# Graph network on one core: one-hots stored and loaded, maxima taken on 32 rows, the edge angle by TensorE, loops written out

## What is computed

```python
def transformer_conv(x, src, dst, edge_attr, Wq, bq, Wk, bk, Wv, bv, We, Wskip, bskip):
    ...
    e = (edge_attr @ We).reshape(-1, HEADS, C)
    k_j = k[src] + e
    v_j = v[src] + e
    alpha = jnp.einsum('ehc,ehc->eh', q[dst], k_j) / jnp.sqrt(jnp.float32(C))
    amax = jax.ops.segment_max(alpha, dst, num_segments=n)
    expa = jnp.exp(alpha - amax[dst])
    denom = jax.ops.segment_sum(expa, dst, num_segments=n)
    attn = expa / (denom[dst] + 1e-16)
    out = jax.ops.segment_sum(attn[:, :, None] * v_j, dst, num_segments=n)
...
rel_t = last_update[src] - t
rel_t_enc = jnp.cos(rel_t[:, None] * Wt[0][None, :] + bt)
edge_attr = jnp.concatenate([rel_t_enc, msg], axis=-1)
```

## Time and profile before

| | us |
| --- | --- |
| median of 3 runs | 13423.76 |
| lowest and highest | 13402.09, 13431.12 |
| span of the profiled execution | 13400.0 |
| preparation, to the first layer | 1505 |
| attention passes over the edges (four) | about 1150 each |
| gated pass over the edges | 1418 |
| convolution passes over the edges | 1673 and 1686 |

### The profile page before, as it was taken

One profiled execution on the slowest core, in us unless ns is written; L12 is line 12 of the kernel. 1 busy time (PEld: TensorE's weight loads), 2 busy tenths in 40 slices (PEclk: granted clock), 3 DMA queues, 4 the chain that ended last, 5 costly groups with the idle time before them and its releaser, 6 DMA issues. The chain is left out here.

```text
span 13400.0 us, 212567 instructions
## 1 busy us (share of the span) xinstructions
PE 8527.8 (64%) x52858; PEld 6962.8 (52%) x52859; DVE 10400.3 (78%) x15015; ACT 3614.6 (27%) x7819; POOL 6926.8 (52%) x7047
## 2 busy tenths in 40 slices
PE   4663477776777677775465652777266666567764
PEld 3553245554455535654455542555266666566664
DVE  8666569974799748996688875888778888688888
ACT  0111133332333233332244431333211111111111
POOL 2775047750477407772277750777145555255553
PEclk8555688877888788887688875666588888788887
DMA  4334754444544474443255550222233334233333
GB/s 182 113 113 119 244 206 106 106 80 193 192 106 106 72 292 123 106 106 53 79 145 145 146 111 19 55 55 54 19 103 106 107 107 105 75 108 105 105 106 72
DMA packets 720185, 1523.62 MB, mean 114 GB/s; under 512 B 364796, under 2 KB 416585, under 8 KB 680627
## 3 DMA queue, kind: packets, MB, share of 16 engines
q0 software_dynamic: 306624, 795.04, 25.0%
q1 hardware_dynamic: 413427, 727.07, 15.9%
HBM read 1050.48 MB, written 471.10 MB: 114 GB/s over the span
## 5 line engine op out<-in xcount | busy, mean ns | idle before, releaser
L970 POOL DMA_INDIRECT h<-table,edges_ring x3984 | 3856.5, 968 | 1889.0 <-issue 1154.3
L1147 PE MATMUL bank<-h,edges_onehot 128*128 128x260 f32 (+1 forms) x7968 | 1986.6, 406 | 652.3 <-issue 469.0
L1147 PEld LDWEIGHTS bank<-h,edges_onehot 128*128 128x128 f32 x7968 | 1570.6, 246 | 978.1 <-issue 717.4
L970 POOL DMA_INDIRECT edges_rows<-table,edges_ring x1512 | 1527.0, 1010 | 716.0 <-issue 431.0
L1122 PE MATMUL bank<-ident,edges_score 128*4 128x128 f32 x5280 | 1027.7, 360 | 1021.5 <-DVE edges_score L1288 737.9
L1258 DVE TENSOR_TENSOR_SCAN bank<-edges_fresh,edges_top,bank 4x1024 f32<-4x1024 bf16 x660 | 1541.5, 2336 | 144.9 <-PE bank L1122 141.2
L1265 DVE TENSOR_TENSOR_SCAN edges_top<-edges_fresh,bank 4x1024 f32<-4x1024 bf16 x660 | 1493.8, 2263 | 0.6 <-issue 0.3
L1122 PEld LDWEIGHTS bank<-ident,edges_score 128*4 128x4 f32 x5280 | 497.6, 104 | 1339.0 <-DVE edges_score L1288 784.9
L1314 DVE TENSOR_TENSOR acc<-acc,bank 128x260 f32 (+1 forms) x2640 | 908.9, 344 | 164.4 <-PE bank L1147 60.4
L2017 POOL DMA_INDIRECT rec<-dst,slots x782 | 797.0, 1019 | 432.7 <-issue 432.4
L1203 ACT ACTIVATE edges_onehotT<-bank 128x1024 bf16<-128x1024 bf16 (+1 forms) x550 | 562.1, 1022 | 1153.3 <-PE bank L1087 715.9
(11 more groups left out here) (346 smaller groups left out, 18152.3 us busy)
## 6 DMA issues: line engine op xcount, KB each, us to landing
table<-x SPq DMA_DIRECT2D x154, 1040.0 KB, 7.9
edge_score<-edge_feat SPq DMA_DIRECT2D x220, 512.0 KB, 3.8
table<-h SPq DMA_DIRECT2D x77, 1040.0 KB, 7.9
table<-source_typed_rows SPq DMA_DIRECT2D x63, 1040.0 KB, 8.1
h<-table,edges_ring POOLq DMA_INDIRECT x3984
edge_feat<-edge_score SPq DMA_DIRECT2D x110, 512.0 KB, 2.9
dst_row<-dst_rows SPq DMA_DIRECT2D x71, 704.0 KB, 4.2
buf<-rec SPq DMA_DIRECT2D x44, 840.0 KB, 5.2
```

The costliest lines, as they stand in the source:

```text
L970: pool.indirect_dma_start(out=rows[s % R][:, j, :], out_offset=None, in_=table, in_offset=bass.IndirectOffsetOnAxis(ap=ring[:, s * ST + j: ...
L1147: ins = pe.matmul(sum_b[k % 3], onehot[s][:, j, :], rows[s][:, j, A0:W], start=j == k * GT, stop=j == (k + 1) * GT - 1)
```

## The change

**Loops.** Every `Fori` over superblocks and over the chunks of the ranking becomes a Python loop, so that all 110 superblocks stand in the instruction stream one after the other. The order within the four attention passes is the same. `load_bin` stays.

**Gated pass.** SP stores each one-hot and its transpose to two tables in HBM, `onehot_d` and `flip_d` (two DMAs of 512 KB for a superblock). The angle is made by PE: rel (with a column of ones) is transposed, and one matmul with `angle_w` gives rel times `wt` plus `bt`, in turns. DVE then has two operations on 512 columns in place of seven. The one-hot of the next superblock is flipped a turn ahead; feature transposes come a turn later. The four `load_bin` of DVE stand together behind the weighting.

**Convolutions.** A new function `conv_edges` takes the place of `attention_edges(conv=...)`. One-hots are neither made nor transposed: SP loads both with the features (three DMAs of 512 KB for a superblock, where it was one). Each half has its own PSUM bank, and it is spread one turn ahead of its use. The maxima are taken with the scores turned to 32 rows (4 heads times 8 tiles) of 128 edges: `find_ends` reduces, PE lines the 32 ends up on one row, `link` scans that row in both directions, PE turns the result back as start values, and `scan_both` scans 32 rows of 128. The marks of segment starts that this needs are computed once, in the preparation, and stored.

```diff
+def stages(engine, step, depth):
...
+    for i in range(NSUPER + depth - 1):
+        static(i)
...
+def conv_edges(g, name, conv):
...
+                def load_features(p):
+                    u, s = number(p), p[1] % 2
+                    hold(sp, half_ready, 2 * (u - 1))
...
+                    sp.dma_start(feat[s], g.edge_feat[:, bass.ds(u * (ST * P), ST * P)]).then_inc(feat_in[s], 16)
+                    sp.dma_start(onehotT[s], g.flip_d[:, bass.ds(u * (ST * P), ST * P)]).then_inc(feat_in[s], 16)
...
+                    hold(sp, sums_made, GPS * (u - 1))
...
+                    sp.dma_start(onehot[s][:, :], g.onehot_d[:, bass.ds(u * (ST * P), ST * P)]).then_inc(onehot_in[s], 16)
...
+                def line_up(m):
...
+                    for k, last in enumerate((ends[:, 0:1], ends[:, 1:2], rising[1 - s][:, P - 1:P])):
+                        ins = pe.matmul(line_b, last, g.pick[0:RUNS, k, :], start=k == 0, stop=k == 2)
...
+                def step(p, n, m, o):
+                    if m:
+                        line_up(m)
+                    if o:
+                        sum_group(o, 0)
+                        sum_group(o, 1)
...
+                    if m:
+                        turn_line(m)
+                    if p:
+                        spread_half(p, 0, bins)
...
+                    if o:
+                        sum_group(o, 2)
+                        sum_group(o, 3)
+                    if m:
+                        turn_top(m)
+                    if p:
+                        spread_half(p, 1, bins)
+                    if n:
+                        turn_scores(n)
...
+                def find_ends(m):
...
+                    for k, at in enumerate((2 * P + 1, 0)):
+                        ins = v.tensor_tensor_reduce(masked[:, k, :], score_b, marks[s][:, at:at + P], 1.0, -BIG,
+                                                     ALU.add, ALU.max, ends[:, k:k + 1])
...
+                def step(p, n, m, o):
+                    if m:
+                        find_ends(m)
+                    if n:
+                        convolve_half(n, 0)
...
+                        add_sums(o, 0, bins)
+                        add_sums(o, 1, bins)
+                    if m:
+                        link(m)
+                    if n:
+                        convolve_half(n, 1)
...
+                    if m:
+                        scan_both(m)
+                    if n:
+                        make_score(n)
+                    if o:
+                        add_sums(o, 2, bins)
+                    if m:
+                        subtract_top(m)
+                    if o:
+                        add_sums(o, 3, bins)
+                    if m:
+                        weigh_rows(m)
+                stages(v, step, 4)
...
+                def store_onehot(q, s):
...
+                    sp.wait_ge(flipped_kept, u + 1)
...
+                def step(n, o, more=True):
+                    if n:
+                        spread(n, load_bins(pe, g, number(n)))
+                    if o:
+                        sum_group(o, 0)
+                        sum_group(o, 1)
+                    if n:
+                        turn_rel(n)
+                    if o:
+                        flip_features(o)
+                    if n:
+                        make_angle(n)
+                    if n and more:
+                        flip_onehot(after(n))
+                    if o:
+                        sum_group(o, 2)
+                        sum_group(o, 3)
...
+                        bins = load_bins(v, g, w)
...
+                        c.link(v.tensor_scalar(turns, angle_b, 12582912.0, 12582912.0, ALU.add, ALU.subtract))
...
+                        v.tensor_tensor(angle, angle_b, turns, ALU.subtract).then_inc(angle_made, 1)
...
-        attention_edges(g, "edges31", table3, src_idx, conv=1)
+        conv_edges(g, "edges31", 1)
```

## The result

| | before | after |
| --- | --- | --- |
| median of 4 runs, us | 13416.78 | 12858.53 |
| lowest and highest | 13402.09, 13431.12 | 12858.11, 12866.06 |
| span of the profiled execution | 13400.0 | 12856.3 |

A forecast was written before the change was run, and what follows sets the result against it. POOL was taken to bound the attention passes, DVE and its handovers with PE the convolutions, DVE with POOL close behind the gated pass. 13400 - 438 - 451 - 126 + 22 = 12407 us, plus 24 gives 12431 us; range 12200 to 12800.

The forecast's parts named there:

- DVE's work: DVE's busy time per superblock: 13.1 - 6.0 + 2.0 = 9.1 us in a convolution, 8.0 us in the gated pass.
- DVE's waiting in the convolutions: Convolutions: 1.8 us of waiting kept per superblock, largest at the maxima and the weighting behind ACT's chain.
- The two pairs of bins: Convolutions: two pairs of bin loads, one operation ahead of each, costed at nothing, or 0.6 us a pair otherwise.
- PE's term: Convolutions: PE busy 10.5 - 4.0 + 0.9 = 7.4 us per superblock, treated as cover.
- The rival of the low clock: Convolutions and gated pass: PE granted 1.2 GHz throughout, giving 13048 us in all; chance 0.08.
- The end of the passes: Convolutions: the last superblocks get their rows late, adding 0.1 us per superblock when spread over the pass.
- Gated pass: Gated pass: fewer DVE operations but bins in a row at 1.6 us; 11.6 us per superblock, 126 us off.
- POOL as second limit: Gated pass: POOL's time of 10.7 to 11.7 us per superblock, near DVE's 11.1, as a second limit.
- Preparation: Preparation: DVE makes the marks, about 11 us, and SP stores them, 11 us; 22 us added.
- Attention passes: Attention passes: at POOL's pace with unchanged instructions, so no gain and no loss from written-out loops.
- The rival of the code: Written-out loops: some 850 more code blocks stop the pipeline, 13706 us at 1.5 us per block; chance 0.05.
- DMA as a limit: Gated pass and convolutions: DMA engines can't go above 0.75 with gathers in the mix, 12617 us; chance 0.12.

The follow-up runs named there:

- gb_cs: Changed kernel with DVE's gated-pass bin loads each behind its own operation, and all four convolution sums in a row ahead of the spread; 12377 us (0.9230).
- c_fill: Changed kernel with added PE multiplications of the identity by itself where PE waits in the convolutions; 12629 us (0.9414).
- gs_cl: Changed kernel with gated-pass third and fourth sums ahead of the transposes, and convolution features multiplied by 8 of 128 weight columns; 13493 us (1.0065).
- pad_rank: Changed kernel with empty places gathering from different table rows and the ranking's chunk loop a loop again; 12634 us (0.9424).
- g_old: Changed kernel with the gated pass in its old form and order, plus the two new stores; 12742 us (0.9501).
- rank_loop: Changed kernel with the ranking's chunk loop a loop again, on a slower chip; 15036 us, kernel before there 15215 us.

## Why the prediction was wrong, step by step

- **DVE's work** (13.1 - 6.0 + 2.0 = 9.1 us, gated 8.0): right, 8.9 and 8.2. A masked reduction takes 0.28 and 0.07 us, a link scan 0.19, a scan of 128 columns 0.48, within a tenth of the values taken.
- **DVE's waiting in the convolutions** (1.8 us kept, at the maxima and ACT's chain): the step that failed. It is 12.0 - 8.9 = 3.1 us, 1.5 of it for the sums (165.7 us over the pass at line 1676), some 0.4 at the weighting, 0.5 for gathered rows, most of it at the two ends of the pass. The cause of the largest part is PE, which the prediction had put down as cover only: undoing the order on PE takes two thirds of this wait away, and 173 us off the first convolution (153 off the second). The two pairs of bins that it cost at nothing did cost next to nothing.
- **PE's term** (7.4 us): mis-sized, and twice; PE is busy 9.2 us. Matmul records overlap, so each moment is counted here for one of them only. The transpose of scores and the eight small products take 1.6 us, not 0.9: most are two records in the trace, of 0.17 to 0.27 us each, however narrow. And the matmuls of the spread, which did not change, take 5.3 us instead of 4.1, since they now fall where the clock is low (0.81 at them instead of 0.98). These two, 0.7 and 1.2, are the whole of the miss. The 4.0 us that PE loses is right counted this way, with the transposes of line 1135 that the sum left out. gb_cs and c_fill show what order and clock are worth: 1171 and 1237 us, where the forecast had 1235.
- **The rival of the low clock** was the right mechanism, at the wrong place and scale. It was thought of as a clock of 0.5 throughout, for 13048 us, with a chance of 0.08. What happened is a mix at nearly the same mean (0.84 to 0.81) whose low part moved into the spread ahead of the sums. Where the clock did fall that far, in gs_cl (0.51), the first convolution took 1720 us and not the 1390 that this rival had worked out for it. A mean granted clock of a pass says nothing on which instructions get it. The Trainium skill, TensorE: Matmul & The Clock Gate, section "HAM oscillation — how this bites in real kernels", describes a kernel whose every round waits for data, falls to the low clock and starts cold; the timeline from 10533 agrees, with a pause of 4.14 us and a spacing of 0.43 us after it. The lighter matmuls of gs_cl show a case that such a wait does not explain.
- **The end of the passes** (0.1 us a superblock, 11 us): six steps of 16.1 us are some 26 us more than six at 11.8, and pad_rank took 38 and 31 us off. The cause given, rows that come late, was right, and its size less than half; why they are late (one row of the table for all) was not seen.
- **Gated pass** (-126): DVE's bins were taken at 1.6 us; what shows as issue before line 1975 is (178.0 + 58.0) / 110 = 2.1 us a step (58.0 for the 27 steps on the fourth ring buffer), and undoing the row gave 131 us. The ends of 0 and 3.5 held it. What the sum left out is the sums' new place behind the transposes (236 us of waiting, 108 us when undone). The loop's turns, costed at nothing, were worth some 52 us here in the change's favour, which hid more than half of the loss: against g_old the new form costs 86 us. That the pass came out no more than 160 us off its forecast is in part luck.
- **POOL as second limit** (10.7 to 11.7 us): it is busy 8.5 us with 2.3 us of gaps, 10.8 together, and waits for PE's sums, so it was not what held the pass. The prediction set aside the rule of the Trainium skill on the shared port (SBUF — State Buffer, section "Who interferes with whom") because the mean cost was less than half of the operation's length. Read gather by gather, the trace of the gated pass agrees with it. An undisturbed gather takes 0.946 us. The 90 that start with 0.87 us left of a DVE operation with both inputs in SBUF take 1.69 us, the 71 that start with 0.24 us left take 1.05. POOL, when it comes second, is held for about what is left of the operation; the prediction's 3.7 us took each operation at its full length. The other way round nothing shows: DVE operations that start inside a gather keep their 1.22 us.
- **Preparation** (22 us): the marks cost about 25. The ranking was missed by 45 us. No instruction of it changed but the loop, and rank_loop's edit in pad_rank gave all of it back (1035 us). The scatter takes 58 ns longer on average, and 782 of them make up the 45 us; why it does was not followed.
- **Attention passes** (0): 3.5 us longer each, 15 in all. The written-out code costs at most this: 781 blocks more, and POOL's pace hides the rest. The rival of the code falls, and this agrees with the rule of the Trainium skill that the prediction cited (Runtime: NRT & Kernel Launch, section "Instruction fetch mechanics"). In the ranking and the gated pass writing out a loop moved the time by +45 us, all of it in the scatters' own durations, and by some -52 us.
- **DMA as a limit**: its share is 0.73 and 0.74, and gb_cs reaches 0.82 at 252 GB/s. The limit of 0.75 in that rival does not exist here.

The misses in the spans are 211 us in the convolutions, 160 in the gated pass, 51 in the preparation and 15 in the attention passes, 437 of the 449 between 12407 and 12856. The remaining 12 lie in the node-wise work.

## What to carry to other kernels

Before a PE with gaps is called cover, ask what stands on its queue ahead of the result that another engine waits for, and price that at the low clock: here two sums behind eight matmuls of the spread (16 records) cost DVE 1.5 us of waiting a step, and putting them ahead took 173 us off. The mean granted clock of a pass is not enough for this; read it at the instructions in question. Making TensorE's matmuls narrow can make a pass slower (376 us); a few matmuls added where PE waits, in a bank that is free then, are a cheap test of whether the clock is the cause (107 us), but they cost time once PE is nearly full (48 us). DVE's register loads belong one behind each long operation (131 us), and filler entries of an index list should not all name the same row (187 us).

## What the runs showed of the hardware that was not expected

- Granted clock and time go together, against the amount of work: the first convolution took 1344 us at 0.81, 1237 at 0.94 with 1516 matmul records (seven matmuls a step) added, and 1720 at 0.51 with the least work for the array.
- One program differs by 13% from chip to chip (13412 against 15188 to 15215 us for the kernel before), and on the slower ones the event that PE's transposes are done comes 2.75 us after their record at the median instead of 0.23. A change that is worth 4.2% on one kind is worth 0.9% on the other.
- Gathers whose 128 descriptors all read one row take 0.42 us a packet instead of 0.16.
- A gather that POOL starts beside a DVE operation with both inputs in SBUF takes longer by about what is left of that operation (1.69 us with 0.87 us left, 0.946 alone).
- Four register loads in a row behind an operation with both inputs in SBUF took 2.63 us of DVE's time; the first two took 0.90 us each at the median, the last two 0.30. The Trainium skill, DMA: Bandwidth & Descriptors, section "Latency and other measured facts", gives about 600 ns as the floor of such a load; the trace shows 0.30 us for the shortest and 0.53 at the median of these rows, and about 0.6 for a short one only with the register instructions behind it.
